# Pair-ordered keys, an earlier first projection, a reordered routing stage and another place for the last wait, in a one-core perceiver block

## The chip, the cores and the metric

The kernel runs on one core of a Trainium2 chip. The metric is the device time of one execution in microseconds (us); every time below is in us unless marked otherwise. PE is TensorE, DVE is VectorE, ACT is ScalarE, POOL is GpSimd, SP is SyncE. A q behind a name (SPq, POOLq) is that engine's instruction sequencer.

## What is computed

The input x is 8 sequences of 64 tokens, width 1024: 512 tokens in four tiles of 128. All numbers are fp32. Three residual steps follow each other:

```
x = x + xattn(layernorm(x), ctx, wq, wk, wv, wo)      # 1 head of width 1024, 1601 cached keys + 64 new ones
x = x + attn(layernorm(x), w_qkv, w_out)              # 16 heads of width 64, rope, causal, 64 tokens a sequence
x = x + ffn(layernorm(x), Wg, Wu, Wd, Wr, temperature)

xattn:  q, k_new, v_new = x wq', x wk', x wv';  k = [ctx, k_new];  v = [ctx, v_new]
        softmax(q k' / 32) v, then wo'           # ctx serves as keys and as values
ffn:    inh = sigmoid(x Wr / temperature)        # 8 experts
        weights = exp(-|inh - 1/e| / 0.1) where inh lies in [0.2123, 0.5], else the two nearest; normalised
        out = sum over experts of weights * ((silu(x Wg) * (x Wu)) Wd)
```

## The kernel before, in words

**Units.** All weights and cached keys and values come from HBM in units of 128 x 2048 numbers (1 MB). SP issues the loads in the order in which PE uses the units, into a ring of 4 raw buffers (6 during attention). Each product is made of three single-pass matmuls (fp32r): ACT copies a raw unit to its high part (`split` on ACT, L625), DVE subtracts for the low part (`split` on DVE, L932), and PE sums hi x hi, hi x lo and lo x hi (`three`, L1403 to L1406). SP loads into a raw buffer again once DVE's low part of the unit in it is done (`load`, L421 to L426), and a high buffer is written again once PE has used its unit. Each engine runs its own program in the order written; there is no planner. ACT and DVE split a unit three ahead of the one that PE sums.

**Start.** SP loads the four token tiles (L450 to L453), then the first four weight units. DVE takes the mean and variance of each tile in two halves and a merge (`moments`, L935), ACT the square root (`deviation`), DVE normalises (`normalise`, L941), PE turns the tile in eight 128 x 128 transposes (`norm`, L1408), ACT and DVE take the high and low parts of the turned tile from PSUM, in halves (`transposed_hi`, `transposed_lo`). Then PE sums four units for the queries and four for the new keys, each with 2 x 24 matmuls of all 512 tokens (`stationary_unit`, L1422).

**Attention.** For each of 8 sequences PE scores 7 key units (L1501) and sums 7 value units (L1614). The order of the units is the list `ATTENTION`. Between them PE turns the exponentiated scores of a sequence, 64 rows x 128 columns at a time (`turn_weights`, L1516, L1514 and L1513). A value unit holds cached rows 2p and 2p+1 of a block of 256 in partition p, so that each partition reads 8 KB in one piece. The keys stand in their own order. The turn of chunk kc therefore takes every second column of the scores (L1521). Eight units of the new values' projection are spread among the others.

**Norms 2 and 3.** The out-projection is summed in two halves of 512 columns, tile by tile. DVE adds each half to x (`add`). Half 0 of all four tiles is added first, then two weight units are split, then `add_and_norm` (L1075) adds half 1 of a tile, takes the statistics of the whole tile and normalises it, tile after tile, while PE sums the following tiles and turns the ready ones.

**Routing.** After norm 3, PE sums the router's logits per tile (`logits`) and turns them (`logits_turn`, L1774). ACT copies them in between (`logits_copy`). Then DVE runs a chain of some 60 small steps: sigmoid through Exp, choice of experts, each token's place in its expert's list. PE counts by matmuls with 0/1 matrices. POOL gathers the rows of the first expert's tokens from HBM by an indirect DMA (`gather`, L512), PE turns them (`turn_rows`, L1865).

**Experts.** Each expert has 240 places for tokens, in two groups of 120 rows. PE sums 8 gate and up units and 4 down units; ACT scales the result (L905) and POOL adds it to the output in HBM by four indirect DMAs with addition (`scatter`, L522 to L532). A token list longer than 240 would be handled by extra items after the eighth expert; their number stands in the block `meta`, which DVE computes during the last expert (`overflow`, L1284 to L1317). Every engine reads that number and branches. With this input it is zero.

**End.** POOL waits until all scatters have landed (L539), then until `meta` is ready, reads it, branches, and all engines meet at a barrier (told as L184 in the profile).

Of the kernel before, what the change touches and what calls it, by code (L numbers as in the profile page):

```python
# [9 lines left out]
ACT = mybir.ActivationFunctionType  # L10
# [172 lines left out]
def perceiver_block(nc, x_d, ctx_d, keys_d, tail_d, w_d, wr_d, temp_d, ident_d, rope_d, route_d, count_d, out_d):  # L183
    with ExitStack() as ctx:  # L184
# [235 lines left out]
        def _(sp):  # L420
# [33 lines left out]
            for k in range(RING):  # L454
                load(k, w_d[k])
# [20 lines left out]
            with sp.If(more > 0):  # L476
                with sp.Fori(0, more) as j:
                    e = sp.value_load(meta[0:1, bass.ds(j + 1, 1)], min_val=0, max_val=NE - 1)
                    for k in range(PER_EXPERT):
                        load(U_FFN + NE * PER_EXPERT + k, w_d[PER_EXPERT * e + (W_FFN + k)], PER_EXPERT, j)  # L480


        @block.gpsimd
        def _(pool):
# [50 lines left out]
            for e in range(NE):  # L535
                if e + 1 < NE:
                    gather(e + 1)
                scatter(e)
            pool.wait_ge(scattered, 64 * NE + 16)  # L539
            pool.wait_ge(meta_ready, 1)  # L540
            more = pool.value_load(meta[0:1, 0:1], min_val=0, max_val=MORE)
# [63 lines left out]
        def _(act):  # L605
# [38 lines left out]
            def norm(n):  # L644

                for t in range(TT):
                    if t > 0:
                        transposed_hi(n, t - 1)
                    deviation(n, t)
                if n == 2:  # L650
                    logits_copy(0)
                    logits_copy(1)
                transposed_hi(n, TT - 1)

            act.wait_ge(eps_set, 1)
            for t in range(TT):
                deviation(0, t)
            for t in range(TT):
                transposed_hi(0, t)
                if t > 0:  # L660
                    split(t - 1)
# [204 lines left out]
            split(U_FFN + 2)  # L866


            act.activation(small[:, 14, 29:30], eps[:, :], ACT.Exp).then_inc(y_done, 1)
# [4 lines left out]
            act.activation(small[:, 6, :], small[:, 4, :], ACT.Exp, scale=-1.0 / 0.3).then_inc(edist_ready, 1)  # L874

# [44 lines left out]
        def _(dve):  # L920
# [14 lines left out]
            def moments(t):  # L935
                for h in range(2):
                    steps.done(dve.bn_stats(stats[:, t, h, :], x[:, t, h * HALF:(h + 1) * HALF]))
                steps.wait()
                dve.bn_aggr(mv[:, t, :], stats[:, t, :, :].rearrange("p h n -> p (h n)")).then_inc(stats_ready, 1)
# [19 lines left out]
            for t in range(TT):  # L959
                dve.wait_ge(x_loaded[t], 16)  # L960
                moments(t)
                if t in (1, 2):
                    normalise(0, t - 1)
            for t in range(TT):
                transposed_lo(0, t)
                if t < 2:
                    normalise(0, 2 + t)
                if t > 0:
                    split(t - 1)
# [105 lines left out]
            def add_and_norm(n, base, out, bank):  # L1075

                for t in range(TT):
                    add(base, out, bank(t), 1, t)
                    dve.wait_ge(evacuated, base + TT + t + 1)
                    moments(t)  # L1080
                    if t > 0:
                        transposed_lo(n, t - 1)
                    normalise(n, t)
# [5 lines left out]
            split(U_QKV)  # L1089
            split(U_QKV + 1)  # L1090
# [88 lines left out]
            split(U_FFN)  # L1179
            split(U_FFN + 1)  # L1180
            add_and_norm(2, E_WOUT, O_WOUT, lambda t: t % 2)
            split(U_FFN + 2)
# [99 lines left out]
            slot_values()  # L1282

# [115 lines left out]
        def _(pe):  # L1399
# [71 lines left out]
            for t in range(TT):  # L1471
                norm(0, t)
            pe.wait_ge(ln_lo, 2 * TT)
            for k in range(U_KEYS0):
# [41 lines left out]
            def turn_weights(s):  # L1516

                pe.wait_ge(p_ready, s + 1)
                for kc in range(NCH - 1):
                    n = P if kc < 12 else KREM  # L1520
                    columns = bass.ds(2 * P * (kc // 2) + kc % 2, P, step=2) if kc < 12 else slice(KFULL, KV)  # L1521
# [486 lines left out]
```

## Time and profile before

| | |
|---|---|
| median of 3 runs | 1290.64 us (1289.09 to 1295.51) |
| the profiled execution's own time | 1296.42 us |
| its span, first to last instruction | 1294.6 us |
| mean granted TensorE clock | 0.975 of full speed |
| busy: PE / DVE / ACT / POOL | 94% / 63% / 49% / 7% |
| chain that ended last, by engine | PE 79%, DVE 7%, ACT 5%, issue 4%, DMA 4% |
| DMA | 272.98 MB, 210 GB/s over the span |

The profile was taken on one execution whose own time lies above the median of the runs. Durations below come from it. "Busy" for PE includes overlapping matmuls: two matmuls that follow each other at full rate overlap in the profile, and only the distance of their starts tells the pace.

The stages by time in the span: start to 26, query and key projections to 117, attention to 444, its out-projection with norm 2 to 500, self-attention to 675, norm 3 and routing to 732, experts to 1285.

### The profile page before, as it was taken

To read this page: it belongs to the slowest core of one execution; us is meant where nothing else is said; L and a number is where in the kernel's file an instruction comes from. 1 tells how busy PE (TensorE), PEld (TensorE's weight loads), DVE (VectorE), ACT (ScalarE), POOL (GpSimd) and SP (SyncE) were. 2 spreads that over 40 slices of the span, in tenths; PEclk is the share of its full clock that TensorE was granted. 3 is DMA by queue.
4 is the path that set the end of the run, shared out by engine and by line. 5 is a ranking of instruction groups with operands and counts; after the bars stand their busy time and mean duration, and the time that the engine had idled before them with its cause. 6 is when DMAs were issued, how large, how long until landed. Compare 5 with 4: busy or idle time off the path is not lost.

```text
span 1294.6 us, 19218 instructions
## 1 busy us (share of the span) xinstructions
PE 1215.7 (94%) x7762; PEld 1061.1 (82%) x7762; DVE 819.7 (63%) x1026; ACT 633.6 (49%) x604; POOL 95.8 (7%) x74
## 2 busy tenths in 40 slices
PE   4999999999998999999997599999999999999996
PEld 3887777777777888888886598989899999999894
DVE  7335788988998547464566474746565565656464
ACT  4113788888897423114543244444444445454440
POOL 0011000000000000000000011121111111121201
PEclk9999999999999899999999699998999999999998
DMA  8254889999999544220244176765766767676632
GB/s 296 97 179 150 299 324 366 366 362 360 381 368 328 180 177 163 98 98 33 94 152 168 51 258 193 229 207 171 216 207 221 214 208 211 216 215 225 192 131 33
DMA packets 46872, 272.98 MB, mean 211 GB/s; under 512 B 5880, under 2 KB 6024, under 8 KB 18528
## 3 DMA queue, kind: packets, MB, share of 16 engines
q1 hardware_dynamic: 36768, 243.48, 51.8%
q0 software_dynamic: 10048, 28.71, 9.2%
q8 instruction: 40, 0.66, 0.2%
q14 instruction: 16, 0.13, 0.0%
HBM read 255.92 MB, written 16.25 MB: 210 GB/s over the span
## 4 chain that ended last, share of the span: by engine, by line
PE 79%; DVE 7%; ACT 5%; issue 4%; DMA 4%; POOL 0%; SPq 0%; ACTq 0%; DVEq 0%; POOLq 0%
PE ps L1404 21%; PE ps L1405 21%; PE ps L1406 21%; PE ps L1501 6%; DVE lo L932 4%; DMA out<-y,target 3%; ACT hi L625 3%; PE ps L1614 2%; PE ps L1865 1%; PE ps L1549 1%; PE ps L1514 1%; ACT scores L687 1%; PE ps L1707 1%; PE ps L1691 1%; PE ps L1418 0%
## 5 line engine op out<-in xcount | busy, mean ns | idle before, releaser
L932 DVE TENSOR_TENSOR lo<-raw,hi 128x2048 fp32r<-128x2048 f32 (+1 forms) x198 | 443.5, 2252 | 171.7 <-ACT hi L625 169.4
L625 ACT ACTIVATE hi<-raw 128x2048 fp32r<-128x2048 f32 (+1 forms) x198 | 370.5, 1881 | 263.8 <-PE ps L1406 254.9
L1404 PE MATMUL ps<-act_hi,hi 128*128 128x240 f32 (+1 forms) x1216 | 359.3, 296 | 10.9 <-DVE act_lo L955 4.8
L1406 PE MATMUL ps<-act_hi,lo 128*128 128x240 f32 (+1 forms) x1216 | 360.0, 296 | 0.0
L1405 PE MATMUL ps<-act_hi,hi 128*128 128x240 f32 x1024 | 284.4, 278 | 0.0
L1404 PEld LDWEIGHTS ps<-act_hi,hi 128*128 128x128 f32 x1216 | 232.2, 191 | 21.1 <-DVE h_lo L1373 5.2
L1406 PEld LDWEIGHTS ps<-act_hi,lo 128*128 128x128 f32 x1216 | 232.6, 191 | 7.8
L1405 PEld LDWEIGHTS ps<-act_hi,hi 128*128 128x128 f32 x1024 | 195.3, 191 | 0.3
L1404 PE MATMUL ps<-hi,act_hi 128*128 128x512 f32 x320 | 126.2, 394 | 0.0
L1406 PE MATMUL ps<-hi,act_lo 128*128 128x512 f32 x320 | 124.8, 390 | 0.0
L1405 PE MATMUL ps<-lo,act_hi 128*128 128x512 f32 x320 | 124.6, 389 | 0.0
L897 ACT ACTIVATE xq<-ps 128x240 f32<-128x240 f32 x64 | 23.8, 371 | 168.6 <-PE ps L1406 168.5
L1501 PE MATMUL ps<-hi,qs 128*128 128x512 f32 (+1 forms) x256 | 94.7, 381 | 7.7 <-DVE lo L932 5.1
L1404 PE MATMUL ps<-hi,h_hi 128*128 128x512 f32 x256 | 101.2, 395 | 0.0
L1405 PE MATMUL ps<-lo,h_hi 128*128 128x512 f32 x256 | 100.9, 394 | 0.0
L1406 PE MATMUL ps<-hi,h_lo 128*128 128x512 f32 x256 | 100.9, 394 | 0.0
L1614 PE MATMUL ps<-hi,pt 128*128 128x512 f32 (+1 forms) x208 | 87.0, 418 | 6.0 <-DVE lo L932 5.0
L1501 PE MATMUL ps<-lo,qs 128*128 128x512 f32 (+1 forms) x256 | 91.7, 373 | 0.0
L1614 PE MATMUL ps<-lo,pt 128*128 128x512 f32 (+1 forms) x208 | 83.5, 401 | 0.0
L932 DVE TENSOR_TENSOR lo<-raw_more,hi 128x2048 fp32r<-128x2048 f32 (+2 forms) x38 | 76.8, 2032 | 9.8 <-ACT hi L625 9.8
L1405 PE MATMUL ps<-act_lo,hi 128*128 128x512 f32 x192 | 75.3, 392 | 0.0
L529 POOL DMA_INDIRECT out<-y,target x32 | 51.8, 1618 | 307.0 <-ACT y L905 304.7
(228 smaller groups left out, 1449.6 us busy)
## 6 DMA issues: line engine op xcount, KB each, us to landing
raw<-weights SPq DMA_DIRECT2D x124, 1024.0 KB, 5.0
raw<-keys SPq DMA_DIRECT2D x36, 1024.0 KB, 5.5
raw<-context SPq DMA_DIRECT2D x31, 1024.0 KB, 7.5
raw_more<-context SPq DMA_DIRECT2D x17, 1024.0 KB
raw_more<-keys SPq DMA_DIRECT2D x12, 1024.0 KB
xq<-x_in SPq DMA_DIRECT2D x4, 512.0 KB, 6.5
raw_more<-weights SPq DMA_DIRECT2D x4, 512.0 KB
new_keys_t<-kvs POOLq DMA_DIRECT2D x8, 256.0 KB, 3.2
```

The lines of the kernel that those rows point to most:

```text
L529: pool.indirect_dma_start(out_d.rearrange("t (g d) -> (t g) d", g=2), bass.IndirectOffsetOnAxis(ap=target[0:R, g, n:n + 1], axis=0), y[0:R ...
L625: act.activation(part(hi, k, kind), part(raw, k, kind), ACT.Copy).then_inc(hi_done, 1)
L687: act.activation(S[rows, :], S[rows, :], ACT.Exp, bias=nb[rows, :], scale=SCALE, accum_out=sums[rows, :]).then_inc(p_ready, 1)
L897: act.activation(silu[:, k % 2, :], ps[:, k % 2, 0:CAP], ACT.Silu).then_inc(silu_done, 1)
L932: dve.tensor_tensor(part(lo, k, kind), part(raw, k, kind), part(hi, k, kind), ALU.subtract).then_inc(lo_done, 1)
L1404: pe.matmul(out, a_hi, b_hi, start=first, stop=False)
L1405: pe.matmul(out, a_hi, b_lo, start=False, stop=False)
L1406: return pe.matmul(out, a_lo, b_hi, start=False, stop=last)
L1501: ins = pe.matmul(scores_at(j, slice(0, P)), qs[:, s % 2, cc, :], buf[:, k % RING, c * w:(c + 1) * w], start=(cc == 0 and b == 0), stop=(c ...
L1514: return pe.transpose(out, S[rows, columns], ident[rows, rows])
L1549: ins = pe.matmul(out, O[:, c * P:(c + 1) * P], twice[:, 0:QL], start=True, stop=(s < LATE))
L1614: ins = pe.matmul(ps[:, 6 + h, :], pt[rows, kc, :], buf[rows, k % RING, at], start=(kc == 0 and b == 0), stop=(kc == NCH - 2 and b == 1))
```

## The change

1. Keys of each block of 256 are stored by the host in pair order (first the even ones, then the odd ones), so that a turn reads 128 neighbouring columns of the scores.
2. At the start, the first weight unit is loaded behind two token tiles and in front of the other two. All engines handle tiles 0 and 1 first, then split unit 0. PE sums unit 0 for the first 256 tokens (two groups of 24 matmuls of 256 columns, norms of tiles 2 and 3 between them), then for the other 256.
3. In norms 2 and 3 DVE takes the statistics of half 0 of all tiles between the two weight splits, and only those of half 1 in the chain of a tile.
4. In routing, ACT's and DVE's splits of unit U_FFN + 2 move behind the exponentials and behind `slot_values`. The small Exp that makes ACT load its table moves between the logits copies of tiles 0 and 1.
5. POOL no longer waits for the scatters before the branch. It waits for `meta` and reads it ahead of the last expert's four scatters. SP waits for all scatters at its end.

The diff, cut:

```diff
@@ sync
             for t in range(TT):
                 sp.dma_start(x[:, t, :], x_d[t * P:(t + 1) * P, :]).then_inc(x_loaded[t], 16)
                 ...
+                if t == 1:
+                    load(0, w_d[0])
-            for k in range(RING):
+            for k in range(1, RING):
                 load(k, w_d[k])
 ...
+            sp.wait_ge(scattered, 64 * NE + 16)
@@ gpsimd
             for e in range(NE):
                 if e + 1 < NE:
                     gather(e + 1)
+                else:
+                    pool.wait_ge(meta_ready, 1)
+                    more = pool.value_load(meta[0:1, 0:1], min_val=0, max_val=MORE)
                 scatter(e)
-            pool.wait_ge(scattered, 64 * NE + 16)
-            pool.wait_ge(meta_ready, 1)
-            more = pool.value_load(meta[0:1, 0:1], min_val=0, max_val=MORE)
@@ scalar
                 if n == 2:
                     logits_copy(0)
+                    act.activation(small[:, 14, 29:30], eps[:, :], ACT.Exp).then_inc(y_done, 1)
                     logits_copy(1)
 ...
-            for t in range(TT):
-                deviation(0, t)
-            for t in range(TT):
-                transposed_hi(0, t)
-                if t > 0:
-                    split(t - 1)
+            deviation(0, 0)
+            deviation(0, 1)
+            split(0)
+            transposed_hi(0, 0)
+            transposed_hi(0, 1)
+            deviation(0, 2)
+            deviation(0, 3)
+            split(1)
+            transposed_hi(0, 2)
+            transposed_hi(0, 3)
+            split(2)
 ...
-            split(U_FFN + 2)
-            act.activation(small[:, 14, 29:30], eps[:, :], ACT.Exp).then_inc(y_done, 1)
             act.wait_ge(z_ready, 1)
 ...
             act.activation(small[:, 6, :], small[:, 4, :], ACT.Exp, scale=-1.0 / 0.3).then_inc(edist_ready, 1)
+            split(U_FFN + 2)
@@ vector
-            for t in range(TT):
+            for t in range(2):
                 dve.wait_ge(x_loaded[t], 16)
                 moments(t)
-                if t in (1, 2):
-                    normalise(0, t - 1)
 ...
+            normalise(0, 0)
+            normalise(0, 1)
+            split(0)
+            transposed_lo(0, 0)
+            transposed_lo(0, 1)
+            for t in range(2, TT):
+                dve.wait_ge(x_loaded[t], 16)
+                moments(t)
+            normalise(0, 2)
+            normalise(0, 3)
+            split(1)
+            transposed_lo(0, 2)
+            transposed_lo(0, 3)
+            split(2)
 ...
                     dve.wait_ge(evacuated, base + TT + t + 1)
-                    moments(t)
+                    moments(t, first=1)
 ...
             split(U_QKV)
+            for t in range(TT):
+                dve.wait_ge(evacuated, O_WO + t + 1)
+                half_stats(t, 0)
             split(U_QKV + 1)
 ...
             split(U_FFN)
+            for t in range(TT):
+                dve.wait_ge(evacuated, E_WOUT + t + 1)
+                half_stats(t, 0)
             split(U_FFN + 1)
             add_and_norm(2, E_WOUT, O_WOUT, lambda t: t % 2)
-            split(U_FFN + 2)
 ...
             slot_values()
+            split(U_FFN + 2)
@@ tensor
+            def half_tokens(j, h):
+                cols = slice(h * TOK // 2, (h + 1) * TOK // 2)
+                for c in range(C):
+                    at = slice(j * D + c * P, j * D + (c + 1) * P)
+                    ins = three(ps[:, j, cols], hi[:, 0, at], lo[:, 0, at], act_hi[:, c, cols], act_lo[:, c, cols],
+                                c == 0, c == C - 1)
+                return ins
+
-            for t in range(TT):
-                norm(0, t)
+            norm(0, 0)
+            norm(0, 1)
+            unit_ready(0)
+            pe.wait_ge(ln_lo, TT)
+            half_tokens(0, 0)
+            norm(0, 2)
+            norm(0, 3)
+            half_tokens(1, 0)
             pe.wait_ge(ln_lo, 2 * TT)
-            for k in range(U_KEYS0):
+            for j in range(2):
+                half_tokens(j, 1).then_inc(out_ready, 1)
+            for k in range(1, U_KEYS0):
 ...
-                    columns = bass.ds(2 * P * (kc // 2) + kc % 2, P, step=2) if kc < 12 else slice(KFULL, KV)
+                    columns = slice(kc * P, (kc + 1) * P) if kc < 12 else slice(KFULL, KV)
@@ host
-    keys = context[:, :KFULL].reshape(B, 3, HALF, 2, 4, P).transpose(0, 1, 3, 5, 4, 2).reshape(B, 6, P, UNIT)
+    in_pairs = context[:, :KFULL].reshape(B, 6, P, 2, D).transpose(0, 1, 3, 2, 4).reshape(B, KFULL, D)
+    keys = in_pairs.reshape(B, 3, HALF, 2, 4, P).transpose(0, 1, 3, 5, 4, 2).reshape(B, 6, P, UNIT)
```

## Rows read from the trace of the kernel before

**Rows 1.** Busy time by stretch: stretch, its length, each engine's busy time (instructions), PEclk, DMA.
```profile
480.00:505.00 25.00, 25.00 (x128) 21.03 (x127) 16.09 (x27) 8.84 (x13) 0.55 (x1) 1.00 0.24 98
682.00:727.00 45.00, 23.70 (x213) 20.67 (x211) 26.12 (x80) 9.93 (x21) 4.41 (x6) 0.80 0.40 140
```
**Rows 2.** The four loads of the token tiles (L451): issue and landing.
```profile
L451 SPq DMA_DIRECT2D xq<-x_in x4: 395/428/432, 0.7 to 2.6; - x4
...
DMA to landing us min/median/max: 3.7/6.5/7.7
```
**Rows 3.** Instructions in time, start: start, length, engine, line, tiles, count [idle before].
```profile
7.82 1.28 DVE L937 BATCH_NORM_STATS2 stats<-xq 128x6 f32<-128x512 f32 x2 [1.86 <-DMA xq<-x_in]
...
16.12 1.93 ACT L625 ACTIVATE hi<-raw 128x2048 fp32r<-128x2048 f32 x1
...
24.66 1.28 DVE L955 TENSOR_TENSOR act_lo<-ps,act_hi 128x512 fp32r<-128x512 f32 x2
...
26.00 0.79 PE L1404 MATMUL ps<-act_hi,hi 128*128 128x512 f32 x1 [4.83 <-DVE act_lo L955]
```
**Rows 4.** Busy time by stretch, for PE's pace: first matmuls, projections, first expert.
```profile
27.00:29.00 2.00, 2.00 (x6) 1.59 (x5) 2.00 (x3) 0.00 (x0) 0.00 (x0) 1.00 0.94 397
...
40.00:100.00 60.00, 60.00 (x266) 49.68 (x265) 21.37 (x17) 10.34 (x6) 4.27 (x5) 1.00 0.40 136
...
740.00:750.00 10.00, 9.97 (x89) 9.77 (x88) 8.06 (x14) 7.26 (x6) 0.00 (x0) 1.00 0.43 141
```
**Rows 5.** Weight loads of two kinds of turns by form (busy, mean ns); chain in attention.
```profile
L1514 PEld LDWEIGHTS ps<-ident,scores 64*128 64x128 f32 x88 | 11.6, 219 | 0.0
...
L1691 PEld LDWEIGHTS ps<-ident,qk 128*128 128x128 f32 x64 | 7.2, 141 | 0.5
...
229.41 1.36 PE ps L1514 x12
```
**Rows 6.** Instructions in time, norm 2: DVE, and PE's first turn.
```profile
471.49 4.49 DVE L932 TENSOR_TENSOR lo<-raw,hi 128x2048 fp32r<-128x2048 f32 x2 [1.32 <-ACT hi L625]
475.89 0.69 DVE L1073 TENSOR_TENSOR xq<-ps,xq 128x512 f32<-128x512 f32 x1
...
478.71 0.81 DVE L947 TENSOR_SCALAR head_scores<-xq,mv,rstd 128x1024 f32<-128x1024 f32 x1
...
480.16 1.03 PE L1418 MATMUL ps<-ident,head_scores 128*128 128x128 f32 x8
```
**Rows 7.** Instructions in time, routing: ACT, PE and DVE.
```profile
700.15 0.27 ACT L641 ACTIVATE xq<-ps 8x128 f32<-8x128 f32 x1 [1.78 <-PE ps L1406]
...
705.18 0.38 PE L1774 MATMUL ps<-ident,xq 8*128 8x8 f32 x2 [0.36 <-ACT xq L641]
...
706.95 1.28 ACT L869 ACT_TABLE_LOAD   x1
706.96 2.29 DVE L932 TENSOR_TENSOR lo<-raw,hi 128x2048 fp32r<-128x2048 f32 x1 [4.34 <-ACT hi L625]
...
710.13 0.25 DVE L1205 TENSOR_SCALAR small<-ps,small 128x32 f32<-128x32 f32 x1
...
729.20 2.99 DVE L1350 TENSOR_TENSOR act_hi<-ps,act_hi 128x480 fp32r<-128x480 f32 x4 [5.37 <-ACT act_hi L880]
```
**Rows 8.** End: gathers, meta, chain, last scatter, and sequencer rows (ns min/median/max, first, last start).
```profile
721.42 1.00 POOL L518 DMA_INDIRECT rows<-x_norm,source  x1 [0.30 <-issue]
...
1278.47 0.18 DVE L1317 CAST meta<-small 128x17 int32<-128x17 f32 x1
...
1279.73 0.80 issue
...
1283.26 1.61 POOL L529 DMA_INDIRECT out<-y,target  x1 [1.12 <-DMA out<-y,target]
...
L541 POOLq TENSOR_LOAD <-meta x1: 502/502/502, 1288.2 to 1288.2; - x1
...
L184 POOLq DRAIN  x1: 5213/5213/5213, 1289.2 to 1289.2; - x1
```

## What I expected, before the change was run

> **What bounds the kernel now.** I read the page first (busy shares), then the stretches, then the instructions in order of time where the edits fall, last the issuing engines' own instructions at the end. PE is busy 94% of the span by the page, without a gap for 25 us around the layer norm after attention, and for 23.70 of 45 us in routing [rows 1]. So an edit is worth something where PE waits: at the start, in attention's weight turns, in routing, and behind the last matmul. Elsewhere only harm can come: what makes PE wait counts in full.
>
> The sum is made against the profiled execution (span 1294.6, own time 1296.42). That lies 5.8 above the median of the runs, 1290.64; I take the differences over to the median.
>
> **Start: 5.9 us off.** Before, PE's first projection matmul starts at 26.00 [rows 3], behind all four token tiles. It runs at 1.2 GHz for about 3.15 us (6 matmuls of 512 columns touch 27 to 29, two cut by an edge, 0.43 each; the granted clock reads 1.00 there, the pace shows the lower level), then at 2.4 GHz, 266 in 60 us or 0.23 [rows 4]. 48 matmuls: 8 x 0.40 (to 29.2) + 40 x 0.23, so unit 1 begins at 38.4.
> After: tiles 0 and 1 are there as before (tile 1's statistics begin at 7.82 [rows 3]). W0 now stands where x2 and x3 stood: the same bytes, so it lands when x3 did, issued at 2.6 + 7.7 = 10.3 [rows 2]. x2 and x3 follow at about 11.6 and 12.9 (half a megabyte each at the 397 GB/s of rows 4). Then one after the other: ACT splits W0, 1.9 (12.3); DVE its low part, 2.3 (14.6), while ACT copies four halves; DVE four low halves at 0.61 (1.28 for two with their overlap), 2.45 (17.1) [rows 3]; PE's first 24 half matmuls. 240 columns take 0.11 at full clock (89 in 10 us [rows 4]), so 256 take 0.118 and about 0.22 at half: 15 at 0.22 + 9 at 0.118 = 4.4 (21.5). DVE meanwhile: two tiles' statistics 2.9 and two normalisations 1.75 (21.7), low part of W1 behind ACT's split (24.4), four low halves 2.45 (26.8). PE's other work (16 transposes, 24 half matmuls) fits before 26.8. Then 48 x 0.118 = 5.7: unit 1 begins at 32.5 instead of 38.4. W1 to W3 keep their places behind the same bytes, and W0's slot is free for W4 earlier. From there to the projections' end PE is never idle (60.00 of 60 [rows 4]), so 5.9 stays. Bounds: W0 landing as late as an unmoved queue would give, 2.6 later (3.3 gained); all halves at half clock, 5 more (0.9); W0 early, about 7.
>
> **Key order: 3.6 off, the least certain term.** The strided turns have a weight load of 219 ns; contiguous turns of the same 128 columns load in 141 [rows 5]. Twelve turns take 1.36, 0.113 each. Contiguous ones take 0.109, but move 128 columns and not 64. If the load was the limit, a turn falls to about 0.06: 12 x 0.053 = 0.6 a step. Six such rows stand on the chain that sets the end (one stands in rows 5), so 3.6. If 0.109 is a floor, 12 x 0.004 x 6 = 0.3. I take the first, since the load is nearest in kind to row L1691's. That these rows are links of the chain says that PE's own work ends last there.
> The Trainium skill (TensorE: Matmul & The Clock Gate, section LDWEIGHTS) has the load cost by columns alone, columns/1.2 ns, an estimate of 107 ns for both orders; by that the term is 0.3. SBUF — State Buffer in the Trainium skill (Door 1: The DMA port swizzle) lets four-byte data stride up to four elements free, again 0.3. The 141 against 219 of rows 5 does not agree with either. Rival A below is the case of these two rules.
>
> **First halves of the statistics: 1.35 + 1.35 lost, 0.65 gained.** Each statistics instruction is 0.65 (1.29 for two). After attention, DVE is busy without a break from 471.49: two splits (4.49), then the add at 475.89, one block late for it; the normalised tile ends at 479.52 and PE turns it at 480.16 [rows 6], 0.64 of slack. Four half statistics (2.6) now stand between the splits, and the chain behind is 0.65 shorter: ready at 481.5, PE waits 1.35. PE has no gap there to give it back [rows 1]. The same pattern stands at 672.57 to 681.24 in the second norm (1.35). There the last tile's chain, which feeds the router, is 0.65 shorter. Below: the lateness is hidden if DVE is early (0). Above: 2.6 each.
>
> **Routing: 4.5 off.** Before, DVE waits for ACT's split of U_FFN+2, does its low part at 706.96 and five small steps, and takes the logits at 710.13 [rows 7]. PE ends them at 705.18 + 0.38. After, both splits come later, the small steps (about 1 us) beside PE, and DVE takes the logits at 705.65: 4.5. ACT's table load of 1.28 plus 0.2 goes in front of the second logits copy, where ACT idles 1.78 [rows 7], so nothing. The moved DVE split fills the wait for the gathered rows (5.37 idle before 729.20 [rows 7]) against 2.2. SP's next weight load is queued behind it, 12 later, needed some 25 us after that. If the cover is gone, 2.2 of the 4.5 come back.
>
> **End: 1.4 off.** Behind POOL's new wait stand all four scatters of the last expert, two of which went out at 1269 and 1272. The meta block is ready at 1278.65 [rows 8]. POOL's load and checks took 0.75; then 0.82 from the wait's end to the first issue, as before the scatter of 1280.53 [rows 8]: 1280.25. Pitch 1.61 + 0.30 (the gap between two gathers [rows 8]): 1282.2, 1284.1, 1286.0, ended 1287.6. Before, the last was issued at 1283.26, so it is 2.7 later and lands at 1290.8 rather than 1288.1 (wait ended just before the load at 1288.2). What follows in POOL is a DRAIN of 5.21 [rows 8], to 1294.4. It now starts at 1287.7 and ends 1292.9, and with the barrier 1293.2. If that DRAIN counts from the landing, the end is 1297.2, 2.6 worse than before; with a gap of 0.82 for the 0.30 also 1.5 more. If it vanishes when it starts early, 1291.1, 3.5 better. I take a fixed 5.21, the only row of its kind. SP's new wait has nothing behind it but the barrier, and the last landing (1290.8) is over before POOL is.
>
> Sum: -5.9 - 3.6 + 1.35 + 1.35 - 0.65 - 4.5 - 1.4 = -13.35. Profiled 1283.1, median 1277.3.
>
> **Rivals.**
> *A, the key order brings nothing* (0.25): PE's pace in the turns is not the load's. For it, 0.109 in contiguous turns; against, the load times. -10.0: 1280.6. This is also the case that the edit doesn't do what it says.
> *B, the end turns over* (0.17): four late scatters, and DRAIN behind the landing. For it, DRAIN has nothing else to do for 5 us; against, the landing at 1288.1 was already past. End +2.6 instead of -1.4: -9.35, 1281.3; with the long gaps +4.1: 1282.8.
> *C, the start hangs on W0* (0.12): it lands 2.6 later among x2 and x3. For it, the four tiles took 3.7 to 7.7 us to land [rows 2], so they share; against, the same bytes stand before it. -10.7: 1279.9.
> *D, better* (0.06): DVE not late, DRAIN gone: -2.7 - 2.1 more: 1272.5.
> *E, slower* (0.05): PE's clock. The new start has PE wait at 17, 23 and 26 us; if the rise to 2.4 GHz, which before came 3 us into unbroken matmuls, then fails to come, each 512-column matmul costs 0.20 more. It decides from 13.35/0.20 = 67 matmuls, a unit and a half; were it four units, 192 x 0.20 = 38 lost, 1316. Against: full clock came at 29.2 right after a start from rest.
> *The forecast* 0.35.
>
> **Range.** 0.5% is 6.5 us, about what a measurement of this kernel can tell. Each case but E lies over it taken alone, together 0.95; A with the long form of B (-4.5), or with B and part of C, falls inside, for which I take 0.15 off. Faster 0.80, within 0.5% 0.15, slower 0.05. Of the forecast's own terms the sum can move from -18 (D) to about -5 (A and B together, -6.0, and a part of C): 1272 to 1286.
>
> **What would show it.** First projection matmul at about 17, unit 1 at 32.5; twelve turns in about 0.7 rather than 1.36; a PE wait of 1.3 before the first turn of each later norm; logits taken within 0.2 of PE's last; last expert's scatters 1.9 apart from just after the meta block, and a POOL DRAIN of 5.2 from there. The forecast is wrong if turns stay at 0.11, if DRAIN ends 6 us behind the last landing, or if any start row stays at half clock beyond 24 us.

## The result, and the profile after

The changed kernel takes 1279.11 us (median of 5, 1276.98 to 1284.38) against 1290.64 (median of 5), 11.5 us faster; forecast 1277.3. The ratio is 0.9904 [0.9881, 0.9926]. It leaves out each kernel's profiled execution, here and below, and so is not the quotient of the two medians (0.9911). A second set of 6 runs of the same kernel gave 1281.59 (1278.29 to 1289.27) and 0.9921 [0.9895, 0.9947], beside its own runs of before (1292.23). The profiled execution took 1284.38 (span 1282.6, clock 0.975), 12.0 less than that of before; forecast 13.35 less. Times of the changed kernel spread over 7 us in the first set and 11 in the second, so single terms are read from the traces, by the distance between two events, and the times decide only on larger ones. The spread goes with TensorE's granted clock: of the eleven executions, the seven with a mean of 0.979 or more took 1276.98 to 1280.49, the four below it 1282.68 to 1289.27. One execution of the kernel of experiment 6 took 1543.74 us; it is left out, and nothing here explains it.

**Start.** PE's instructions that ended an idle stretch between 16 and 34 (start, length, what, idle before and its releaser), then ACT's first split:

```profile
16.81 0.39 PE L1425 MATMUL ps<-act_hi,hi 128*128 128x256 f32 x1 [3.63 <-DVE act_lo L964]
26.41 0.39 PE L1425 MATMUL ps<-act_hi,hi 128*128 128x256 f32 x1 [0.39 <-DVE act_lo L964]
...
10.04 1.91 ACT L628 ACTIVATE hi<-raw 128x2048 fp32r<-128x2048 f32 x1 [1.19 <-DMA raw<-weights]
```

W0 is there at 10.0 (forecast 10.3), the first projection matmul starts at 16.8 (17), the 48 half matmuls of tiles 2 and 3 at 26.4 (26.8), unit 1 at 32.3 (32.5). [rows 3] had whole matmuls starting at 26.00. POOL's last store of the new keys, the end of this stage, moved from 115.92 to 109.64, by 6.28.

**Turns.** The chain of waits around one sequence's turns (start, length, what), against the 1.36 of [rows 5]; then the weight loads of one sequence, grouped by line (busy, mean ns of one):

```profile
222.93 0.36 PE ps L1550 x2
223.29 0.75 PE ps L1551 x12
224.04 0.17 PE ps L1564 x2
```

```profile
L1551 PEld LDWEIGHTS ps<-ident,scores 64*128 64x128 f32 (+1 forms) x12 | 0.9, 144 | 0.0
```

Twelve turns take 0.75 (forecast 0.7), five times in the chain; the load takes 144 ns, against 141 in the contiguous turns of before ([rows 5]).

**Norm 2.** DVE from the fourth tile's add of half 0 to the first normalised tile, and PE's first turn (answers to [rows 6]):

```profile
460.73 0.69 DVE L1088 TENSOR_TENSOR xq<-ps,xq 128x512 f32<-128x512 f32 x1 [4.75 <-PE ps L1427]
462.74 2.29 DVE L938 TENSOR_TENSOR lo<-raw,hi 128x2048 fp32r<-128x2048 f32 x1 [1.32 <-ACT hi L628]
464.95 2.47 DVE L942 BATCH_NORM_STATS2 stats<-xq 128x6 f32<-128x512 f32 x4
467.33 2.27 DVE L938 TENSOR_TENSOR lo<-raw,hi 128x2048 fp32r<-128x2048 f32 x1
469.52 0.68 DVE L1088 TENSOR_TENSOR xq<-ps,xq 128x512 f32<-128x512 f32 x1
...
471.74 0.81 DVE L956 TENSOR_SCALAR head_scores<-xq,mv,rstd 128x1024 f32<-128x1024 f32 x1
...
472.61 0.66 PE L1439 MATMUL ps<-ident,head_scores 128*128 128x128 f32 x4 [1.03 <-DVE head_scores L956]
```

The wait that was forecast (1.3) is there, 1.03, and another of 1.03 at 674.93 in norm 3. The first row shows what was overlooked: DVE idles 4.75 ahead of the fourth tile's add, with three tiles' halves ready.

**Routing** (answers to [rows 7]): DVE takes the logits, and the first expert begins.

```profile
695.71 0.22 DVE L1218 CAST count_b<-count_c 128x128 bf16<-128x128 f32 x1
...
698.84 0.25 DVE L1225 TENSOR_SCALAR small<-ps,small 128x32 f32<-128x32 f32 x1 [2.24 <-PE ps L1811]
...
698.35 0.38 PE L1811 MATMUL ps<-ident,xq 8*128 8x8 f32 x2 [0.36 <-ACT xq L644]
716.08 3.43 PE L1902 MATMUL ps<-ident,rows 120*128 120x120 f32 x16 [4.19 <-DMA rows<-x_norm,source]
721.05 0.54 PE L1425 MATMUL ps<-act_hi,hi 128*128 128x240 f32 x1 [1.54 <-DVE act_hi L1371]
```

The small steps now stand before the wait, and DVE takes the logits 0.1 behind PE's last. First turn of norm 3 to the logits: 23.91, before 28.89. The first expert starts 11.38 earlier than before (721.05 for 732.43), so nothing of it came back up to there.

**End** (answers to [rows 8]): the scatters, then the sequencers' last instructions (duration min/median/max in ns, start).

```profile
1270.05 0.69 ACT L911 ACTIVATE y<-ps,target_w 120x512 f32<-120x512 f32 x1 [2.04 <-PE ps L1427]
...
1268.61 1.61 POOL L532 DMA_INDIRECT out<-y,target  x1 [62.29 <-ACT y L911]
1270.52 1.61 POOL L532 DMA_INDIRECT out<-y,target  x1 [0.30 <-issue]
1272.43 1.61 POOL L532 DMA_INDIRECT out<-y,target  x1 [0.30 <-issue]
1274.35 1.61 POOL L532 DMA_INDIRECT out<-y,target  x1 [0.30 <-DMA out<-y,target]
```

```profile
L184 POOLq DRAIN  x1: 10804/10804/10804, 1271.5 to 1271.5; - x1
...
L184 SPq DRAIN  x1: 13/13/13, 1279.9 to 1279.9; - x1
```

The scatters are 1.91 apart, as forecast. SP is past its wait at 1279.9, but DRAIN ends at 1271.5 + 10.8 = 1282.3, 6.35 behind the last scatter's recorded end (1275.96); forecast was 5.3. From the start of the last scaled rows (the ACT row) to the span's end it is 12.55, before 12.88: 0.3 in this pair, where 1.4 was forecast. This pair flatters the new end. In the other five traces that have it (experiments 1, 2, 5, 6 and 7) the same distance is 13.0 to 13.2, and the mean of all six, 12.99, is that of the old end (12.88 here, 12.99 in experiment 4). So the new end brings nothing that the traces can show.

The account between equal events of the two profiled executions (the reload of x is POOL's load of x after attention; a norm's event is PE's first turn of a normalised tile): start -6.28; attention, to the reload of x, -2.48; norm 2 +1.21; norm 3 +1.24; norm 3 to the logits -4.98; to the first expert -0.09; first expert to the last scaled rows -0.29; end -0.33. Sum -12.0. That the experts' stage is so equal (549.29 and 549.00) is luck: it took 542.0 to 549.3 in the ten traces without the extra matmuls of experiments 9 to 12.

### The profile page after: what moved, and what is told of

It is laid out like the page before. It is cut to its first block, busy times and chain, and to the rows that moved or that the text cites. A ratio compares the mean times of both kernels' runs of the same rounds, so it can differ in the third digit from the quotient of the medians.

```text
span 1282.6 us, 19314 instructions
## 1 busy us (share of the span) xinstructions
PE 1211.0 (94%) x7810; PEld 1059.3 (83%) x7810; DVE 819.6 (64%) x1026; ACT 633.5 (49%) x604; POOL 95.7 (7%) x74
## 4 chain that ended last, share of the span: by engine, by line
PE 76%; DVE 9%; ACT 6%; issue 4%; DMA 3%; POOLq 0%; POOL 0%; SPq 0%; ACTq 0%; DVEq 0%
PE ps L1425 20%; PE ps L1426 20%; PE ps L1427 20%; PE ps L1538 6%; DVE lo L938 4%; ACT hi L628 3%; DMA out<-y,target 2%; PE ps L1651 2%; PE ps L1902 1%; PE ps L1586 1%; DVE stats L942 1%; ACT scores L696 1%; DMA raw<-weights 1%; PE ps L1744 1%; PE ps L1728 1%
## 5 line engine op out<-in xcount | busy, mean ns | idle before, releaser
L1425 PE MATMUL ps<-act_hi,hi 128*128 128x240 f32 (+2 forms) x1232 | 362.0, 294 | 10.0 <-DVE h_lo L1394 4.2
L1427 PE MATMUL ps<-act_hi,lo 128*128 128x240 f32 (+2 forms) x1232 | 363.0, 295 | 0.0
L1427 PEld LDWEIGHTS ps<-act_hi,lo 128*128 128x128 f32 x1232 | 236.1, 192 | 6.9
L1426 PE MATMUL ps<-act_lo,hi 128*128 128x512 f32 (+1 forms) x208 | 78.3, 376 | 0.0
```

Source lines behind the costliest of these rows:

```text
L1425: pe.matmul(out, a_hi, b_hi, start=first, stop=False)
L1426: pe.matmul(out, a_hi, b_lo, start=False, stop=False)
L1427: return pe.matmul(out, a_lo, b_hi, start=False, stop=last)
```

## The experiments

All are edits of the changed kernel; times are medians, and the ratio is to the kernel before, run in the same set. That kernel's median was 1290.97 in the set of experiments 1 to 4, 1292.15 in that of 5, 6, 8 and 9, 1292.23 in that of 7, 10 and 11 and 1292.46 in that of 12, so medians of different sets compare to no better than some 2 us. The stretch "keys to x" is from the last store of the new keys to the reload of x, that is, all of attention.

**1. Keys in their own order again** (keys_old). The host's order is undone with it; the edit, cut:

```diff
-                    columns = slice(kc * P, (kc + 1) * P) if kc < 12 else slice(KFULL, KV)
+                    columns = bass.ds(2 * P * (kc // 2) + kc % 2, P, step=2) if kc < 12 else slice(KFULL, KV)
```

> The changed kernel with the keys in their own order and the strided turns again, all else as changed. Theory (the weight load of a strided turn sets its pace): the twelve turns of a step take 1.36 again instead of 0.75, five or six such steps stand in the chain, so attention is 3.1 to 3.6 longer; the changed kernel's attention was only 2.5 shorter, and the theory puts the missing 0.6 on the clock between the first and the second sequence, which then reads as in the kernel before. Median 2.5 to 3.6 over the changed kernel's, about 1282. Rival A (the order brings nothing to the end, the 2.5 came from elsewhere, as from the clock): turns 1.36 but no more than 0.3 in attention's end.

1282.68 us, 0.9926 [0.9908, 0.9945]. The chain has

```profile
222.54 1.36 PE ps L1551 x12
```

and five more such rows. From the second sequence's turns to the reload of x: 253.49 against 250.26 in the changed kernel, 3.23, of which 5 x 0.61 are turns in the chain. Rival A falls. Over all traces keys to x is 328.7 and 328.4 with the old order and 323.7 to 327.6, mean 325.4, in ten with the new (experiments 10 and 12, which edit attention, left aside): 3.2. The times agree as far as they reach: 3.6 over the first set of the changed kernel, 1.1 over the second.

**2. Statistics whole again** (stats_whole): `half_stats(t, 0)` is removed between the splits, and `moments(t, first=1)` is `moments(t)`.

> The changed kernel with the statistics of both halves in each tile's chain again, all else as changed. Theory (four half statistics ahead of the second weight split make DVE late for the first tile of norms 2 and 3, and that is all they do there): the PE wait of 1.03 before the first turn of each of the two norms is gone, -1.2 and -1.2; the logits come 0.65 later; together 1.7 faster than the changed kernel, about 1277.4. Rival (PE's wait there is DVE's lateness from the weight splits, which the shorter chains behind merely move): the waits stay and the kernel is 0.6 slower than the changed one.

1277.80 us, 0.9887 [0.9864, 0.9909].

```profile
472.45 0.40 PE L1421 MATMUL ps<-hi,act_lo 128*128 128x512 f32 x1
472.69 1.03 PE L1433 MATMUL ps<-ident,head_scores 128*128 128x128 f32 x8
```

(PE, norm 2, in order of time.) PE goes into the turns without a wait. Reload of x to norm 2's first turn: 35.55 for 36.74; from there to norm 3's: 201.07 for 202.32; from there to the logits: 24.44 for 23.91. 1.19 + 1.25 - 0.53 = 1.9 faster, as the theory has it.

**3. The read of the meta block behind the last scatter** (end_last).

```diff
-                else:
-                    pool.wait_ge(meta_ready, 1)
-                    more = pool.value_load(meta[0:1, 0:1], min_val=0, max_val=MORE)
                 scatter(e)
+            pool.wait_ge(meta_ready, 1)
+            more = pool.value_load(meta[0:1, 0:1], min_val=0, max_val=MORE)
```

> The changed kernel with POOL's wait for the meta block and its read behind the last expert's fourth scatter instead of ahead of the first; POOL still does not wait for landings, SP does. The last scatter then goes out 1.5 after the last scaled rows, as in the kernel before, about 2.6 earlier than in the changed kernel. Theory (POOL's DRAIN ends a set time behind its last instruction, or 2.8 behind the last landing): it follows, and the time from the last scaled rows to the end of the span falls from 12.5 to 9.2 to 9.9: 2.6 to 3.3 faster. Rival (the 10.8 of the changed kernel's DRAIN record is its price whenever DMAs are outstanding, counted from its own start): 13.5 to 15.5 from the last scaled rows, 1 to 3 slower.

1275.45 us, 0.9879 [0.9854, 0.9904].

In the chain of waits ACT's last scaled rows start at 1263.87; from there to the end of the span it is 9.5 instead of 12.55. These are the last two scatters, then the sequencers:

```profile
1262.68 1.61 POOL L532 DMA_INDIRECT out<-y,target  x1 [6.79 <-ACT y L910]
1265.41 1.61 POOL L532 DMA_INDIRECT out<-y,target  x1 [1.12 <-DMA out<-y,target]
```

```profile
L184 POOLq DRAIN  x1: 6648/6648/6648, 1266.5 to 1266.5; - x1
...
L184 SPq DRAIN  x1: 13/13/13, 1270.7 to 1270.7; - x1
```

DRAIN ends 6.13 behind the last scatter, so the 10.8 was no price of its own. It ends 2.4 behind SP's pass, as in the changed kernel.

**4. POOL's end as before** (end_old): wait for the landings, wait for meta, read; SP waits for nothing.

> The changed kernel with POOL's end as before: it waits for the scatters' landing, then for the meta block, reads it, branches; SP waits for nothing. Theory (what the new end brings is small, since its last scatter leaves 2.7 later than before and gives that back): from the last scaled rows to the end of the span 12.9 as before against 12.5, so 0.3 slower than the changed kernel, not to be told from it by the times; DRAIN 5.2. Rival (DRAIN with nothing outstanding is shorter or longer here): more than 1 off that in either direction.

1278.47 us, 0.9895 [0.9871, 0.9918]. Last scatter at 1265.94, span 1277.4: 11.46 behind it, as before (11.34), with a DRAIN of 5.21 from 1272.0. From the last scaled rows it is 12.99, as expected; but the changed kernel's mean of six is 12.99 too. The times can't tell the two apart.

**5. The start as before** (start_old).

> The changed kernel with the start as before (four token tiles, then the weight units; all tiles' norms, then whole matmuls), all else as changed. Theory (the first unit's 24 half matmuls run beside the last two tiles' norms, and nothing later takes the gain back): the last store of the new keys comes 6 later again, at 115.5 to 116, and stays 6 later to the end: median 5.9 to 6.3 over the changed kernel's, about 1285. Rival (part of the gain is given back behind the first stage, at loads that now come too late or at the clock's dip between the first two sequences): 3 to 4 over it.

1284.72 us, 0.9940 [0.9919, 0.9961]. The last store of the new keys came at 117.11, later than the 115.5 to 116 expected; in the old start of this execution the first 13 whole matmuls went at half pace and not 7 (PE, in order of time):

```profile
31.22 0.63 PE L1412 MATMUL ps<-act_hi,hi 128*128 128x512 f32 x1
31.65 0.52 PE L1413 MATMUL ps<-act_lo,hi 128*128 128x512 f32 x1
32.01 0.39 PE L1414 MATMUL ps<-act_hi,lo 128*128 128x512 f32 x1
```

In twelve traces with the new start that store lies within 108.9 to 109.9, mean 109.4; in the changed kernel's profile PE came to full pace at 20.4, before the last tiles were ready. So the old start is 7.7 behind at the last store here, where the first pair had 6.3, and 6 x 0.20 = 1.2 of it are the six further slow matmuls. At the reload of x it is 5.9 behind the mean of nine with the new (440.86 for 435.0): attention took 323.75 in this execution, at the low end of the 323.7 to 327.6 of the others. Whether these 1.8 are chance or given back, one trace can't tell; 5.9 is above the rival's 3 to 4 either way. The medians differ by 5.6 and, against the second set, by 3.1, so the times alone don't decide it.

**6. The splits and the small Exp in routing as before** (route_old).

> The changed kernel with the splits of unit U_FFN + 2 and the small Exp at their old places, all else as changed. Theory: from the first turn of norm 3 to DVE's taking of the logits 4.4 to 4.5 more than in the changed kernel's 23.9, and nothing of it comes back before the first expert matmul. The first expert then starts as late after the end of PE's steady work as before: if it is this distance that set how long the first expert ran at the lower clock, 15 rather than 27 of its matmuls go at 0.213, so the difference at the end is no larger than 3.3; if the clock's rise there has no tie to it, 4.5. Median 3.3 to 4.5 over the changed kernel's, about 1283.

1285.08 us (median of five), 0.9939 [0.9917, 0.9960]: 6.0 over the changed kernel's first set, 3.5 over its second. First turn of norm 3 to the first expert: 50.60 for 46.12, 4.48. DVE again takes the split first:

```profile
700.14 2.29 DVE L938 TENSOR_TENSOR lo<-raw,hi 128x2048 fp32r<-128x2048 f32 x1 [4.34 <-ACT hi L628]
702.35 0.22 DVE L1219 CAST count_b<-count_c 128x128 bf16<-128x128 f32 x1
```

20 of the first expert's matmuls went at 0.21, before it was 15, in the changed kernel 27, in end_last none. In the eight traces with the shorter routing and no extra matmuls it is none in four and 18 to 27 in four, in the two with the longer 15 and 20. So that number isn't tied to routing's length.

**7. The changed kernel once more** (after_again).

> The changed kernel once more, unaltered, to have its times beside the others of this call and a second trace of it. Theory (the unequal stage lengths of the first comparison, 2.5 and not 3.1 to 3.6 in attention and 1.2 given back in the first expert, are moments at which the clock rises and falls, which differ between executions of one program): the same 1276 to 1284 in the times, but other lengths in those two stages: between the last store of the new keys and the reload of x anything from 323.7 to 327.6, slow first expert matmuls anything from 0 to 27. Rival (they belong to the change): 326.2 and 27 again, within 0.3 and 3.

1281.59 us. Its trace gave 326.31 for keys to x and a slow first expert again, so by itself it speaks for the rival. But end_last, whose instructions up to there are the same, had none slow, and end_old, the same again, 323.71 for keys to x. Around 720, by stretches, first the changed kernel, then end_last (the granted clock is the third number from the right, 0.50 is 1.2 GHz and 1.00 is 2.4 GHz):

```profile
715.00:720.00 5.00, 3.43 (x16) 3.09 (x16) 1.96 (x3) 2.17 (x4) 0.00 (x0) 0.50 0.58 210
720.00:725.00 5.00, 3.95 (x18) 3.98 (x19) 0.98 (x5) 1.40 (x2) 0.00 (x0) 0.50 0.00 0
```

```profile
715.00:720.00 5.00, 3.43 (x16) 3.09 (x16) 1.97 (x3) 2.24 (x4) 0.00 (x0) 0.53 0.56 210
720.00:725.00 5.00, 4.02 (x36) 4.05 (x37) 0.97 (x4) 1.33 (x2) 0.00 (x0) 1.00 0.00 0
```

With the same work, PE has 18 matmuls in the second stretch or 36. What sets the moment of the rise stays open. So does whether it is each execution or something in each program: the only two traces of one program, after and after_again, agree (27 and 27, 326.23 and 326.31), and the others are of programs that are equal only up to there. That the clock differs between executions of one program is shown by the eleven times above.

**8. Both repairs** (best): the end of experiment 3, and the half statistics where DVE idles. The edit, cut (norm 3 has the same ahead of `add_out(0, 3)`):

```diff
             for t in range(TT):
+                if t == TT - 1:
+                    for u in range(TT - 1):
+                        dve.wait_ge(evacuated, O_WO + u + 1)
+                        half_stats(u, 0)
                 add(O_WO, O_WO, t, 0, t)
...
                     normalise(n, t)
+                    if t == 1:
+                        half_stats(TT - 1, 0)
```

> The changed kernel with two edits: half statistics of tiles 0 to 2 taken ahead of the fourth tile's first add, where DVE idles 4.75, and that of tile 3 where it idles 3.0 behind the second tile's normalisation, in both norms; and POOL's wait and read of the meta block behind the last scatter. Theory: the 1.2 of each norm comes back, the logits keep the 0.65 of shorter chains, the end is 3 shorter: 1.2 + 1.2 + 3 = 5.4 under the changed kernel's 1279.1, so 1273.7. Rival (moved statistics make DVE late somewhere else): the end's 3 alone, 1276.

1274.47 us, 0.9856 [0.9833, 0.9879], between the 1273.7 expected and the rival's 1276; the trace decides.

```profile
454.16 1.87 DVE L941 BATCH_NORM_STATS2 stats<-xq 128x6 f32<-128x512 f32 x3
457.50 0.69 DVE L1087 TENSOR_TENSOR xq<-ps,xq 128x512 f32<-128x512 f32 x1 [1.47 <-PE ps L1429]
459.51 4.49 DVE L937 TENSOR_TENSOR lo<-raw,hi 128x2048 fp32r<-128x2048 f32 x2 [1.32 <-ACT hi L627]
```

The statistics stand in DVE's idle time. Reload of x to norm 2: 35.56; from there to norm 3: 201.08; from there to the logits: 23.84. The first two are those of experiment 2, the last that of the changed kernel: each the better one.

**9. Fillers in routing** (warm): the kernel of 8, with PE matmuls in its idle stretches whose results nobody uses.

```diff
+            def filler(n):
+                for i in range(n):
+                    pe.matmul(ps[:, 6, :], act_hi[:, i % C, 0:P], act_hi[:, i % C, :], start=True, stop=True)
```

> As the kernel of the previous expectation (call it the improved one), with 23 more PE matmuls of 512 columns, whose results nobody reads, in routing: 4 before the first list, 7 before the second, 12 behind it, in PE's idle stretches of 2.1, 3.5 and 4.2. Theory (the first expert's slow start is PE's clock, which rises only under steady work): the turning of the gathered rows and the first expert's first 27 matmuls run at full clock: at least 27 x 0.10 = 2.7 less from the first expert matmul on, and up to 1.5 less in the turns before it. At most 2 can be lost where fillers run past the moment at which the lists or rows are ready. Net 2 to 4 faster than the improved kernel, about 1271. Rival (the clock there doesn't follow PE's idle time): no gain, and up to 2 lost.

1270.34 us, 0.9839 [0.9816, 0.9863], 4.1 less than kernel 8 in the same set; the intervals overlap.

```profile
708.11 4.94 PE L1898 MATMUL ps<-act_hi 128*128 128x512 f32 x12
712.89 1.80 PE L1908 MATMUL ps<-ident,rows 120*128 120x120 f32 x16
716.70 0.35 PE L1427 MATMUL ps<-act_hi,hi 128*128 128x240 f32 x1 [2.00 <-DVE act_hi L1373]
```

The turns take 1.80 for 3.43 and no expert matmul is slow, though the expert starts only 0.7 to 1.1 sooner behind the logits (21.49 for 22.2 to 22.6): ACT and DVE then set the pace. A run without fillers can have no slow expert matmul either, so one trace doesn't price this. From the logits to the last scaled rows it is 564.4 to 571.6, mean 568.2, in ten traces without fillers, and 563.1 to 565.6, mean 564.2, in the four with them (experiments 9 to 12): 4.0 less, and less spread. The turns take 3.43 or 3.44 in all ten and 1.80 to 1.83 in all four.

**10. An earlier copy in attention's first sequence** (newv), on 9.

```diff
                             if b == 0:
+                                new_v_copy(copied)
+                                copied += 1
                                 exps(0)
```

> The kernel with the fillers, and in attention's first sequence ACT's copy of the first block of new values (0.6) moved ahead of its Exp, into 1.4 of idle, instead of behind the next split. Theory: PE's wait of 2.6 before the first turns ends with the Exp at 0.1 to 0.6, and with the wait goes the stretch at the lower clock behind it (0.53 to 0.9 granted for 5 to 10): 2.0 to 5 less from the last store of the new keys to the reload of x, which then takes 319 to 323; median 1266 to 1268.5 against the filler kernel's 1270.3. Rival (PE only waits later, for the weight unit that ACT and DVE split behind the Exp): at most 0.5 less, clock dip as before.

1271.82 us, 0.9854 [0.9826, 0.9883], keys to x 325.28 for kernel 9's 325.32: no gain; the rival held.

```profile
137.35 0.40 PE L1554 MATMUL ps<-ident,scores 64*128 64x64 f32 x2 [0.26 <-ACT scores L695]
137.59 0.91 PE L1555 MATMUL ps<-ident,scores 64*128 64x64 f32 x12
138.34 0.33 PE L1568 MATMUL ps<-cols,twice 64*128 64x1 f32 x2
141.38 0.50 PE L1542 MATMUL ps<-hi,qs 128*128 128x512 f32 x1 [2.72 <-DVE lo L939]
```

The wait of 2.6 only moved behind the turns, for the next unit's low part.

**11. POOL busy behind the last scatter** (drain), on 9: `pool.memset(x[:, 0, :], 0.0)` and the same for `x[:, 1, :]`. One run, 1271.41.

> The kernel with the fillers and two POOL memsets of 128 x 1024 on a tile that is free by then, behind the last scatter and the read of the meta block. They serve nothing, they keep POOL busy for some 2. Read from the trace, from the end of the last scatter's instruction to the end of DRAIN, 6.1 to 6.4 so far. Theory (DRAIN takes 5.2 from POOL's last work, after 0.9 to 1.1 of the scatter that its record doesn't show): that time grows by the memsets' length less what of the 0.9 to 1.1 they cover, by 1 to 2, while SP passes its wait for the landings as before. Rival (DRAIN ends 2.4 to 2.5 behind the moment at which SP has seen the last landing): the memsets are hidden, 6.1 to 6.4 again.

```profile
1260.66 1.61 POOL L532 DMA_INDIRECT out<-y,target  x1 [1.12 <-DMA out<-y,target]
1261.66 1.58 POOL L544 MEMSET xq<- 128x1024 f32 x1
1262.55 1.58 POOL L545 MEMSET xq<- 128x1024 f32 x1
```

```profile
L184 POOLq DRAIN  x1: 7545/7545/7545, 1261.8 to 1261.8; - x1
...
L184 SPq DRAIN  x1: 13/13/13, 1266.0 to 1266.0; - x1
```

DRAIN ends at 1269.35: 5.22 behind the second memset (1264.13), 7.08 behind the scatter where it was 6.04 in kernel 9, and 3.3 behind SP's pass where it was 2.5. The growth of 1.04 is at the lower edge of what was expected, and the rival, that the landing alone sets the end, is out.

That the landing has no part in it is not shown. In the eleven traces in which POOL does not wait for its scatters and has at most the read of `meta` behind them, DRAIN ends 6.0 to 7.05 behind the last scatter's record, but 2.4 to 2.5 behind SP's pass. Two accounts fit all traces: DRAIN takes 5.2 from a true end of the scatter that lies 0.8 to 1.8 behind its record, and the landing follows that end too; or DRAIN ends 5.2 behind POOL's last plain work or 2.4 to 2.5 behind SP's pass, whichever is later. POOL's records are too rough here to tell: the first memset starts at 1261.66, before the scatter's record ends (1262.27).

**12. Fillers in attention's wait too** (warm2), on 9: ten of the same matmuls, into another bank, ahead of `turn_weights(0)`.

> The kernel with the fillers in routing, and ten more PE matmuls of 512 columns that nobody reads, in PE's wait of 2.6 before the first sequence's turns (10 x 0.23 = 2.3 at full clock). The wait itself stays, the turns begin no earlier. Theory (the lower clock of 5 to 10 behind that wait, in every trace so far of 0.53 to 0.90 granted, comes of PE's idleness there): the clock stays at 1.00 from 137 to 152 and the time from the last store of the new keys to the reload of x is 321.5 to 323 instead of 323.7 to 327.6; about 2 less on average, median 1268 to 1269. Rival (the clock falls there whatever PE does, as from the load of ACT, DVE and DMA): 323.7 to 327.6 and the dip again.

1269.46 us (1265.64 to 1272.31), 0.9826 [0.9807, 0.9846], the fastest of all; from kernel 9 the times alone don't tell it. The stretches 142 to 147 of the changed kernel, then of this one:

```profile
142.00:147.00 5.00, 5.00 (x14) 3.98 (x14) 4.94 (x5) 4.93 (x7) 0.00 (x0) 0.53 0.86 311
```

```profile
142.00:147.00 5.00, 4.89 (x21) 3.84 (x22) 4.94 (x6) 4.95 (x7) 0.00 (x0) 1.00 0.99 409
```

The clock stays up, and keys to x takes 321.35, below all ten of before (323.7 to 327.6) and just below the 321.5 expected. It is one trace.

## Why the prediction was right, step by step

- **Start, -5.9: right** (6.3 at the last store in the first pair, 7.7 in experiment 5). The steps came as forecast: W0 0.3 early, 4.4 for the first 24 half matmuls (16.81 to 21.25), DVE's chain 0.4 early. What the forecast took as fixed, 3.15 at half pace in the old start, differs between executions: 7 slow matmuls in one trace, 13 in the other.
- **Key order, -3.6: right in mechanism, 3.2 in size.** Of the six turns counted, the first sequence's ran at the lower clock in the changed kernel and took 1.28 for 1.36. There the contiguous turns come every 107 ns, at full clock every 62, the strided ones at full clock every 113; the recorded loads of the contiguous ones are 231 and 145 ns. The Trainium skill (TensorE: Matmul & The Clock Gate, section LDWEIGHTS) has columns/1.2 ns for a load, 107 here. At full clock it fits neither order, since contiguous turns with a load each come every 62 ns; the 107 ns at the lower clock is the distance of the turns and not the recorded load. Nor is a stride of two free here, as SBUF — State Buffer in the Trainium skill (Door 1: The DMA port swizzle) would have it. The 2.48 of the first comparison was short by chance of the clock: from the second sequence on, behind the clock's fall in the first, it is 3.23 less (experiment 1).
- **Statistics, +1.35, +1.35, -0.65: right** (+1.19, +1.25, -0.53 by experiment 2, +1.9 together for 2.05). The slack was read well; that DVE idles 4.75 just before wasn't used.
- **Routing, -4.5: right** (4.48, experiment 6).
- **End, -1.4: wrong, it is nothing** (0.3 in the first pair; 12.99 for 12.94 from the last scaled rows over six traces with the new end and two with the old). The scatters' times held. The failed step is "What follows in POOL is a DRAIN of 5.21 [...] It now starts at 1287.7 and ends 1292.9": the end was to come 5.3 behind the last scatter's record, and came 6.35 to 7.05 behind it. The one row for it stood behind a wait for the landing, which covered the difference. Whether that is a hidden rest of the scatter or the landing stays open (experiment 11). The last landing was late as well: SP passed 9.85 to 10.5 behind the start of the last scaled rows, where 1290.8 - 1281.7 = 9.1 was forecast.
- **The rivals.** A is out by experiment 1, C by W0 at 10.0, D by the waits of 1.03 and a DRAIN that didn't vanish, E by full pace from 20.4 on. B, as written, had DRAIN take its 5.2 from the landing; it ended 2.4 behind SP's pass, so the end did not turn over. But part of B was there: the landings were late, and the end gave back all that it was to bring.
- **Not in the sum:** the clock's rise in the first expert and its fall in attention and among the experts, up to 4 in attention (323.7 to 327.6) and up to 7 from the first expert matmul to the last scaled rows (542.0 to 549.3). So the sum of right terms can miss a single profile by several us, and that the profiled pair came within 1.4 of the forecast is in part luck.

The five terms by trace: -6.3 - 3.2 + 1.9 - 4.5 + 0 = -12.1 (the start from the first pair); measured -11.5, and in the second set -10.6. The number came out near because the misses are small and lie both ways: start 0.4 better, key order 0.4 and end 1.4 worse.

## What to carry to other kernels

Read where an engine idles just ahead of a chain before work is put into the chain: the half statistics cost 1.9 between two splits and nothing 5 us earlier. A wait that is moved ahead of four queued DMAs should be moved behind them instead, if nothing that they do needs it: from the last scaled rows to the end it is 9.4 to 9.5 then, for 13.0. Where PE waits in the middle of the kernel, count the slow matmuls behind the wait as part of its price; matmuls without use in the wait bought that back here, 4 us on average in routing and the experts behind it.

## What the runs showed of the hardware that was not expected

- The granted clock falls and rises at different moments in traces of programs that are the same up to there: 0 to 27 slow matmuls in the first expert, 323.7 to 327.6 for attention. Extra PE work in the idle stretches brought the rise ahead of the turns in routing in all four traces, and took the fall away in attention in the one trace.
- POOL's DRAIN took 5.21 where its DMAs had landed (two traces) and ended 5.22 behind a memset where they had not (one trace). Behind scatters alone it ended 6.0 to 7.05 after the last one's record and 2.4 to 2.5 after SP had seen the landing (eleven traces).
- A transposed fp32 weight load of 128 columns takes 140 to 145 ns at full clock with neighbouring columns (231 at the lower clock) and 219 ns with every second one. The distance of the turns' matmuls follows it: 62 and 113 ns at full clock, 107 for neighbouring columns at the lower.
